# One graph-convolution layer on one core: multiplied pieces of half a stripe's rows and up to six cells in place of all rows and three cells

## The reference, cut to what matters

```python
h = jnp.maximum(_layernorm(x, axis=-1), 0.0)            # x: 8192 x 128
A_hat = adj + jnp.eye(adj.shape[0])                     # adj: 8192 x 8192, float32, 268 MB
d_inv_sqrt = jnp.sum(A_hat, axis=1) ** (-0.5)
A_norm = d_inv_sqrt[:, None] * A_hat * d_inv_sqrt[None, :]
support = h @ W.T                                       # W: 128 x 128
return x + relu(A_norm @ support)
```

## Time and profile before

| What | Value |
|---|---|
| Median of three runs | 1207.26 us (1203.56 to 1212.42) |
| Profiled execution, span | 1237.8 us, which is its own time from first to last instruction |
| PE, DVE, ACT busy | 983.2, 802.4, 586.5 us |
| Mean PE clock granted | 0.909 of full speed |
| Bytes moved | 391.81 MB, mean 317 GB/s |

### The profile page before, as it was taken

One profiled execution on the slowest core, in us unless ns is written; L12 is line 12 of the kernel. 1 busy time (PEld: TensorE's weight loads), 2 busy tenths in 40 slices (PEclk: granted clock), 3 DMA queues, 4 the chain that ended last, 5 costly groups with the idle time before them and its releaser, 6 DMA issues.

```text
span 1237.8 us, 9242 instructions
## 1 busy us (share of the span) xinstructions
PE 983.2 (79%) x2365; PEld 451.8 (36%) x2365; DVE 802.4 (65%) x965; ACT 586.5 (47%) x1735; POOL 52.6 (4%) x61
## 2 busy tenths in 40 slices
PE   0633346566687788796597999999999999899997
PEld 0631122222233333342243444444444444344443
DVE  5342233444476566575485888888888888778775
ACT  2797587776384637145254451724715653010011
POOL 3000000000000000000000000000000000010001
PEclk9767668678889899998798999999999999999999
DMA  9989999999999999999999999999999997999993
GB/s 301 380 320 309 392 398 362 365 369 347 362 349 343 362 337 322 314 256 274 281 291 278 329 332 360 323 276 333 309 325 320 314 271 215 271 271 348 337 328 88
DMA packets 275204, 391.81 MB, mean 317 GB/s; under 512 B 10832, under 2 KB 252624, under 8 KB 275152
## 3 DMA queue, kind: packets, MB, share of 16 engines
q1 hardware_dynamic: 137648, 195.65, 51.3%
q10 hardware_dynamic: 137504, 195.58, 50.5%
HBM read 386.99 MB, written 4.19 MB: 316 GB/s over the span
## 4 chain that ended last, share of the span: by engine, by line
PE 37%; DMA 8%; ACT 6%; ACTq 3%; DVE 1%; issue 0%; POOLq 0%; SPq 0%; DVEq 0%
PE bank L485 36%; DMA slot<-in_adj_dram 8%; ACT junk L540 6%; ACTq L269 2%; DVE adjT L692 1%; ACTq L277 1%; PE pre L461 0%; ACTq L315 0%; DVE near L778 0%; ACT slot L530 0%; ACT near L558 0%; DVE part L677 0%; POOLq L175 0%; PE sums_bank L449 0%; ACTq L321 0%
## 5 line engine op out<-in xcount | busy, mean ns | idle before, releaser
L485 PE MATMUL bank<-adjT,support 128*128 128x512 f32 x2048 | 936.2, 618 | 152.1 <-DVE adjT L692 150.8
L692 DVE STREAM_TRANSPOSE adjT<-slot 128x1024 f32<-128x1024 f32 x450 | 546.5, 1233 | 268.8 <-DMA slot<-in_adj_dram 157.2
L485 PEld LDWEIGHTS bank<-adjT,support 128*128 128x128 f32 x2048 | 401.8, 199 | 664.6 <-issue 661.0
L540 ACT ACTIVATE junk<-slot 128x384 bf16<-128x384 f32 (+2 forms) x540 | 254.6, 473 | 196.1 <-issue 131.3
L530 ACT ACTIVATE slot<-slot 128x6144 f32<-128x6144 f32 (+11 forms) x64 | 191.8, 2998 | 250.3 <-issue 147.8
L558 ACT ACTIVATE near<-near,dinv 128x128 f32<-128x128 f32 x64 | 20.4, 390 | 177.9 <-issue 88.5
L540 ACT ACTIVATION_READ_ACCUMULATOR junk<-slot 128x1 f32 x540 | 100.8, 187 | 0.0
L692 DVE STREAM_TRANSPOSE adjT<-near 128x1024 f32<-128x1024 f32 x62 | 74.8, 1231 | 19.0 <-PE bank L485 19.0
L540 ACT ACTIVATE junk<-near 128x256 bf16<-128x256 f32 (+1 forms) x192 | 75.5, 394 | 2.8 <-ACT junk L540 2.8
L677 DVE TENSOR_REDUCE part<-slot 128x4 f32<-128x1536 f32 (+2 forms) x45 | 69.0, 1533 | 0.0
L407 POOL TENSOR_TENSOR dinv<-total,power 128x4 f32<-128x4 f32 x16 | 16.1, 1007 | 942.0 <-DVE total L746 942.0
(11 more groups left out here) (53 smaller groups left out, 179.1 us busy)
## 6 DMA issues: line engine op xcount, KB each, us to landing
slot<-in_adj_dram SPq DMA_DIRECT2D x118, 768.0 KB, 15.4
slot<-in_adj_dram ACTq DMA_DIRECT2D x118, 768.0 KB, 13.4
slot<-in_adj_dram ACTq DMA_DIRECT2D x56, 512.0 KB, 11.0
slot<-in_adj_dram SPq DMA_DIRECT2D x56, 512.0 KB, 12.0
slot<-in_adj_dram ACTq DMA_DIRECT2D x12, 1536.0 KB, 15.8
slot<-in_adj_dram SPq DMA_DIRECT2D x12, 1536.0 KB, 17.0
near<-in_adj_dram SPq DMA_DIRECT2D x30, 512.0 KB, 16.8
near<-in_adj_dram ACTq DMA_DIRECT2D x30, 512.0 KB, 15.2
```

Source lines behind the costliest of these rows:

```text
L485: ins = nc.tensor.matmul(bank[bank_of(g)][:], support[:, v * R + t, :], adjT[at % TURNS][:, r, :], start=(n == first_of[g] and t == 0), st ...
L540: nc.scalar.activation(junk[at % JUNKS][:, :n], cells[:, c, :], ACT.Copy, accum_out=part[u % 2][:, k, c:c + 1]).then_inc(junk_done, 1)
L692: nc.vector.transpose(adjT[at % TURNS][:].rearrange("p t (c i) -> p t c i", i=Q), half.rearrange("p c (t r) -> p t c r", r=Q)).then_inc(t_ ...
```

## The change

Left, early and last pieces hold half a stripe's rows (`h`, 256 of 512) and up to six cells (`WIDE`) in place of all rows and up to three. A cell takes two products, one for each half, and each is one transpose of 1024 elements a partition and four matmuls of 256 moving columns into its half of the bank: 16 instructions a cell. The kept cells are loaded by halves. Of the eight row groups of a half DVE sums two and ACT six. Early pieces are those of six cells, from stripe 8 to stripe 14, and the order of the last rows is another. Positions counted in `order` are doubled where they are written as numbers, except `steps`. The small mask tiles for the row sums are made for the new layout once at the start.

```diff
     HALVES = 2
+    WIDE = MOST * HALVES
+    CH = C // HALVES
+    GH = G // HALVES
     TURNS = 3
     BANKS = 5
-    DVE_C = 4
-    FIRST = 4
-    JUNKS = 3
+    DVE_C = 2
+    FIRST = 8
...
     FAR_ROWS = NB - 1 - BAND
-    AGAIN_ROWS = [0, 13, 3, 12, 6, 2, 9, 11, 1, 5, 4, 8, 7, 10]
-    EARLY_TO = 13
+    AGAIN_ROWS = [7, 13, 1, 12, 8, 6, 2, 0, 9, 11, 3, 5, 10, 4]
+    EARLY_TO = 14
     ROW_BANKS = 3
     END_BANKS = [3, 4, 1, 2, 0]
 
-    adj_v = adj.rearrange("(bb u r) (b j) -> u b r bb j", bb=B, u=NB, b=B)
+    adj_v = adj.rearrange("(bb u h r) (b j) -> u h b r bb j", bb=B, u=NB, h=HALVES, b=B)
     adj_far = adj.rearrange("(bb u r) (b j) -> u r bb b j", bb=B, u=NB, b=B)
     x_v = x.rearrange("(b t r) f -> b r t f", b=B, t=NT, r=Q)
...
         n = end - first
-        k = -(-n // MOST)
+        k = -(-n // WIDE)
         return [(first + n * i // k, n * (i + 1) // k - n * i // k) for i in range(k)] if n > 0 else []
...
         left[u] = []
         for v, n in split(0, u):
-            left[u].append(len(landing))
-            landing.append(("left", u, v, n, 0, 0))
+            for h in range(HALVES):
+                left[u].append(len(landing))
+                landing.append(("left", u, v, n, h, 0))
         early[u] = []
         if u <= EARLY_TO:
-            for i in range(u - MOST - BAND - 1, -1, -MOST):
-                early[u].append(len(landing))
-                middle.append((i, u - MOST))
-                landing.append(("again", i, u - MOST, MOST, 0, 0))
+            for i in range(u - WIDE - BAND - 1, -1, -WIDE):
+                middle.append((i, u - WIDE))
                 next_cell[i] = u
+                for h in range(HALVES):
+                    early[u].append(len(landing))
+                    landing.append(("again", i, u - WIDE, WIDE, h, 0))
     AGAIN = len(landing)
     for u in AGAIN_ROWS:
         again[u] = []
         for v, n in split(next_cell[u], NB):
-            again[u].append(len(landing))
-            landing.append(("again", u, v, n, 0, 0))
+            for h in range(HALVES):
+                again[u].append(len(landing))
+                landing.append(("again", u, v, n, h, 0))
 
     slot_of = [m % SLOTS for m in range(len(landing))]
     before_in_slot, landed = [], []
...
-            order.append((i, s, None))
+            for h in range(HALVES):
+                order.append((i, s, h, None))
 
     for s in range(NB):
         stripe_at[s] = len(order)
-        own = [(landing[m][1], v, m) for m in left[s] + early[s] for v in range(landing[m][2], landing[m][2] + landing[m][3])]
-        before = 0 if NB - 1 - s - BAND > 4 else min(FIRST, max(0, s - 1))
+        own = [(landing[m][1], v, landing[m][4], m) for m in left[s] + early[s] for v in range(landing[m][2], landing[m][2] + landing[m][3])]
+        before = 0 if NB - 1 - s - BAND > 4 else min(FIRST, HALVES * max(0, s - 1))
         order += own[:before]
         if s > 0:
             column(s - 1)
         order += own[before:]
     stripe_at[NB] = len(order)
-    rest = [(u, v, m) for u in AGAIN_ROWS for m in again[u] for v in range(landing[m][2], landing[m][2] + landing[m][3])]
+    rest = [(u, v, landing[m][4], m) for u in AGAIN_ROWS for m in again[u] for v in range(landing[m][2], landing[m][2] + landing[m][3])]
     order += rest[:FIRST]
     column(NB - 1)
     order += rest[FIRST:]
-    place = {(u, v): n for n, (u, v, m) in enumerate(order)}
+    place = {(u, v, h): n for n, (u, v, h, m) in enumerate(order)}
 
...
+        return last_final(n) + 10
 
     ctx = ExitStack()
...
         slot = [sb(f"slot{i}", [P, MOST * C * CELL]) for i in range(SLOTS)]
-        near = [sb(f"near{i}", [P, C, 2 * CELL]) for i in range(2)]
-        adjT = [sb(f"adjT{i}", [P, R // HALVES, G]) for i in range(TURNS)]
-        junk = [sb(f"junk{i}", [P, MOST * CELL], mybir.dt.bfloat16) for i in range(JUNKS)]
-        PIECES = max(len(left[u]) for u in range(NB)) + 2
+        near = [sb(f"near{i}", [P, HALVES, CH, 2 * CELL]) for i in range(2)]
+        adjT = [sb(f"adjT{i}", [P, R, GH]) for i in range(TURNS)]
+        junk = [sb(f"junk{i}", [P, WIDE * CELL], mybir.dt.bfloat16) for i in range(JUNKS)]
...
             n = landing[m][3]
-            return slot[slot_of[m]][:, :C * n * CELL].rearrange("p (c j) -> p c j", c=C)
+            return slot[slot_of[m]][:, :CH * n * CELL].rearrange("p (c j) -> p c j", c=CH)
 
         def far_block(m):
...
         def load_cells(queue, quarters, m):
-            kind, u, v, n = landing[m][:4]
+            kind, u, v, n, h = landing[m][:5]
             for b in quarters:
                 queue.dma_start(piece(m)[b * Q:(b + 1) * Q, :, :],
-                                adj_v[u, b, :, :, v * CELL:(v + n) * CELL]).then_inc(ld_slot[slot_of[m]], 16)
+                                adj_v[u, h, b, :, :, v * CELL:(v + n) * CELL]).then_inc(ld_slot[slot_of[m]], 16)
 
         def load_far(queue, quarters, m):
...
         def transposed(n):
 
-            return HALVES * (n + 1)
+            return n + 1
 
...
-            for b in quarters:
-                queue.dma_start(near[u % 2][b * Q:(b + 1) * Q, :, :n * CELL],
-                                adj_v[u, b, :, :, u * CELL:(u + n) * CELL]).then_inc(ld_near[u % 2], 16)
+            for h in range(HALVES):
+                for b in quarters:
+                    queue.dma_start(near[u % 2][b * Q:(b + 1) * Q, h, :, :n * CELL],
+                                    adj_v[u, h, b, :, :, u * CELL:(u + n) * CELL]).then_inc(ld_near[u % 2], 16)
 
         def load_xin(queue, quarters, n):
...
-                for k in range(HALVES):
-                    at = HALVES * n + k
-                    pe.wait_ge(t_done, at + 1)
-                    for r in range(R // HALVES):
-                        t = k * R // HALVES + r
-                        ins = nc.tensor.matmul(bank[bank_of(g)][:], support[:, v * R + t, :], adjT[at % TURNS][:, r, :],
-                                               start=(n == first_of[g] and t == 0), stop=(n == last_of[g] and t == R - 1))
-                    ins.then_inc(used, 1)
+                pe.wait_ge(t_done, transposed(n))
+                for t in range(R):
+                    ins = nc.tensor.matmul(bank[bank_of(g)][:, h * GH:(h + 1) * GH], support[:, v * R + t, :],
+                                           adjT[n % TURNS][:, t, :],
+                                           start=(n == first_of[g] and t == 0), stop=(n == last_of[g] and t == R - 1))
+                ins.then_inc(used, 1)
 
             back = 0
             for s in range(NB + 1):
...
+                    if back < NB and n >= 8 + last_final(back):
                         rows_back(back)
                         back += 1
...
 
-            def late_sums(cells, u, k, before):
+            def late_sums(cells, u, k, h, before):
                 n = cells.shape[2]
-                for c in range(DVE_C, C):
-                    at = before * (C - DVE_C) + c - DVE_C
+                for c in range(DVE_C, CH):
+                    at = before * (CH - DVE_C) + c - DVE_C
                     if at >= JUNKS:
                         act.wait_ge(junk_done, at - JUNKS + 1)
                     nc.scalar.activation(junk[at % JUNKS][:, :n], cells[:, c, :], ACT.Copy,
-                                         accum_out=part[u % 2][:, k, c:c + 1]).then_inc(junk_done, 1)
+                                         accum_out=part[u % 2][:, k, h * CH + c:h * CH + c + 1]).then_inc(junk_done, 1)
 
             def left_sums(m, k, before):
                 act.wait_ge(ld_slot[slot_of[m]], landed[m])
                 next_piece(m)
-                late_sums(piece(m), landing[m][1], k, before)
-                act.wait_ge(junk_done, (before + 1) * (C - DVE_C))
...
+                u, v, h, m = order[n]
                 if m is None:
-                    cells = kept(u, v)
+                    cells = kept(u, v, h)
                 else:
                     dve.wait_ge(ld_slot[slot_of[m]], landed[m])
                     off = (v - landing[m][2]) * CELL
                     cells = piece(m)[:, :, off:off + CELL]
-                for k in range(HALVES):
-                    at = HALVES * n + k
-                    if at >= TURNS:
-                        dve.wait_ge(used, at - TURNS + 1)
-                    half = cells[:, :, k * CELL // HALVES:(k + 1) * CELL // HALVES]
-                    nc.vector.transpose(adjT[at % TURNS][:].rearrange("p t (c i) -> p t c i", i=Q),
-                                        half.rearrange("p c (t r) -> p t c r", r=Q)).then_inc(t_done, 1)
+                if n >= TURNS:
+                    dve.wait_ge(used, transposed(n - TURNS))
+                nc.vector.transpose(adjT[n % TURNS][:].rearrange("p t (c i) -> p t c i", i=Q),
+                                    cells.rearrange("p c (t r) -> p t c r", r=Q)).then_inc(t_done, 1)
                 if m is not None and v == landing[m][2] + landing[m][3] - 1:
```

(10 more changed lines are left out.)

113 lines of the change are left out of this document (64 added, 49 removed).

## The result

The changed kernel takes 1271.03 us, median of 4 runs (1257.31 to 1292.26); the kernel before took 1207.51 in 4 runs beside it. The ratio is 1.0498, 95% interval 1.0458 to 1.0538: **5% slower**, some 60 us by the ratio, and outside the range of the prediction (1192, 1165 to 1224). The profiled execution was the longest of the four, 1292.26 us with a span of 1290.4, in a slow state that the ratio leaves out. The profile of the kernel before (1237.8 us) is also some 30 us above its median.

A forecast was written before the change was run, and what follows sets the result against it. The prediction took loads as the bound up to about 680 us and PE after it. Its terms, -33 + 31 - 19 - 3 + 6 + 3 = -15, turned the median 1207.3 us into 1192, range 1165 to 1224.

The forecast's parts named there:

- Longer packets: Left and early pieces, stripes 8 to 10: mostly 2048 to 3072-byte packets load faster, 395 GB/s for 365; -19 us together.
- rival (a): Packet size is worth nothing, the memory sets the loads' rate: 1211 us, no change; chance 0.24.
- the 59 us above undisturbed rates: Stripes 8 to 10, disturbed load stretches: falls with packet count to 40; about half in a median run, so -10 us.
- Three early cells leave stripes 5 to 7: Stripes 5 to 7, bound by loads, take 46 us each, 138 for 171: -33 us, with PE still covered.
- -33 + 31 - 3 + 6: Early cells leaving stripes 5 to 7, nine more cells from stripe 8 on, stripe 11, and 256-column matmuls, in us.
- 256 columns: PE's matmuls: 4096 instructions for 2048, 0.2174 us each; +6 us, bounds 0 and +9.
- Rival (c): The weight load shows at 256 columns: 1218 us at 0.227 us a start, 1244 at 0.237; chance 0.06.
- PE as the bound from stripe 11: PE full from stripe 11, loads keeping up; stripes 11 to 13 at about 66, 70, 73 us, stripe 14 at 97.
- The last part was to grow by some 20 us: After the last row-sum total: PE multiplies 57 remaining cells for 51, some 20 us longer.
- The chain of totals: Places counted in halved `order` entries make DVE stand at totals: 0.5 us in six last stripes, +3, bounds 0 and +10.
- 66 more issues a queue: More pieces and halved kept loads: 40 us of issues on ACT, which its longer activations save; taken at nothing.
- Rival (b): Slow stretches belong to piece changes, 2.4 us each, +12 us in stripes 8 to 10: 1223 us, slower; chance 0.14.

The follow-up runs named there:

- `cols256`: The kernel before with only its matmuls changed, to 256 moving columns; 1.0022 of the kernel before.
- `after_cut`: The changed kernel with each piece of over three cells loaded in two loads, packets at most 1536 bytes; 1.0465 of the kernel before, median 1259.29 us.
- `plan_cols256`: The kernel before with the new plan (early pieces, order) and matmuls of 256 columns, loads all rows 3 wide as before; 1.0074 of the kernel before, 1215.55 us.
- `after_far`: The changed kernel with each load of a left, early or last piece written to all 128 partitions, output not the reference's; 0.9935 of the kernel before, 1198.37 us.
- `split_both`: `plan_cols256` with each quarter's load of the pieces and of the kept cells split in two; 1.0276 of the kernel before.
- `after_pairs_steps`: The changed kernel with both halves of up to three cells as one piece and the places of the chain of totals doubled; 1.0298 of the kernel before.
- `form_far`: `plan_cols256` with piece loads of up to 3072-byte packets to all 128 partitions, output not the reference's; 0.9757 of the kernel before, 1177.59 us.

## Why the prediction was wrong

**The step that failed is "Longer packets", -19.** It took 395 GB/s for packets of 3072 bytes from one far piece at 401. The far piece writes all 128 partitions; the wide pieces write 32. Alone on the chip they run no faster than 1536 bytes do (326 to 369 GB/s against 357 to 368), and beside other traffic slower. Measured at equal plan and number of loads the form costs +15 us: 34 us off, on the wrong side of both bounds (0 and -40), since I let no reason stand for a loss. The text of rival (a) had the doubt ("a far piece with another target") and gave it no price below nothing. In (a) the Trainium skill ("DMA: Bandwidth & Descriptors", Specifications) has 512 bytes as the least for line rate, and the runs agree with it as far as they go: in each kernel of loads alone, 1536-byte packets (all rows 3 wide) were at most about 1% slower than any form of 3072 into the same partitions.

The other part of that term was the 59 us above undisturbed rates in stripes 8 to 10. To put half of them into a median run was right: in `cols256`, profiled at 1210.1 us, these stripes take 216 us, 29 above the 187. To let them fall with the number of packets was wrong: they are microseconds in which one queue runs far ahead, and with pieces of half the rows there are more of them in the last part (55 us in `after_cut`, 94 in the changed kernel) than with the plan alone (47).

**Three early cells leave stripes 5 to 7: -33.** They took 47, 49 and 53 us, -22 against 171, short of the bound of -27 (the kernel before takes 172 us there in `cols256` too, so these windows can be compared). `plan_cols256` shows the same (46.2, 48.6, 55.3), so it isn't the form: the rate that I took from stripe 4 (369 GB/s) doesn't hold there. In `after_far` the three take 44.8, 43.6 and 49.5, the 138 of the prediction: PE and its clock were indeed covered. As for all of the plan and matmuls, -33 + 31 - 3 + 6 = +1 was forecast, and +9 measured.

**256 columns: +6.** Right: 0.2161 us a matmul, +0.2% alone (-0.1 to +0.5). Rival (c), a visible weight load, is refuted.

**PE as the bound from stripe 11.** Half right. Stripes 12 to 15 took 71, 74, 99 and 60 us, where 70, 73 and 97 were forecast for the first three (`plan_cols256` has 70.3, 73.3 and 96.1); stripe 11 took 71 for 66. The last part was to grow by some 20 us and grew by 53. Six more cells there are 21; the rest is loads that come late. In `plan_cols256` that part takes 222 us with DVE waiting for loads for 7.3 us, so the plan's own growth was forecast rightly; in the changed kernel it takes 251 with 46.1.

**The chain of totals: +3.** The mechanism was right, the size too small: 8 to 13 us. I counted six stripes at 0.5 us. Behind 740 us DVE stood there for 7.1 us in 4 waits, 1.8 each, for 0.9 before; over the whole span it stood 26.4 us for 16.8. With pairs, PE's wait for DVE fell with it when the places were doubled (11.1 to 7.5 us from 640 to 900 us).

**66 more issues a queue: nothing.** The kept loads' split costs about 5 us, if anything. I had priced the issuing engine's time and not the transfers'. Doubling the pieces' loads too would have cost more.

**Rival (b), slow stretches at the change from one piece to the next, when the two queues work on different pieces**, came nearest: slower, 1223. The traces show that it had half of the mechanism. Slow are the stretches in which one queue moves most of the bytes, at some 220 to 260 GB/s into quarters and 359 into 128 partitions; a restart is one occasion for it, and costs 5.4 to 6.3 us into quarters and 2.2 us into 128 partitions. Many changes pass at full rate, as the prediction noted, so its price of 2.4 us a change was an average over unlike cases.

**What adds up and what stays open.** As factors: plan and columns 1.0074, form 1.0119, kept loads 1.0044, chain 1.0068 to 1.0102; their product is 1.031 to 1.034, and the change measured 1.0498. So 1.5 to 1.8%, 18 to 22 us, has no experiment of its own. By another way: `split_both` 1.0276, then 0.2% to `after_pairs_steps`, 1.0% for the chain, and 0.9% from pairs to separate half pieces, which have half as many loads. The 0.2% is well within the intervals. Both ways say that finer order and late loads work together: with the loads to 128 partitions the changed kernel is 1.8% above `form_far`, of which the chain and the kept loads explain 1.1 to 1.5%, so some 0.3 to 0.7% is left for all else. I take it that pieces of half the rows put the queues out of step more often. The counts point that way (55 and 94 us for 47), but `after_cut` and `plan_cols256` differ by only 8 us, and the 94 come from the longest execution of the changed kernel. So this is argued, not shown; what is shown is that DVE waits for late loads there.
